# Last batch of an attention kernel: where the output projections of the batch ahead run, and when the last context is read out

## What is computed

```python
xn  = layernorm(x)                       # x: 8 batches x 512 tokens x 512
q, k, v = split(xn @ Wqkv.T + b_qkv)     # 16 heads of 32
p   = softmax(q @ k.T / sqrt(32) + alibi, causal)
s   = (p @ v) @ Wout.T + b_out           # the output projection, per batch
e   = argmax(xn @ w_router.T)            # one of two experts per token
h   = xn @ w_fc[e].T
a   = square(where(h >= 0, h, 0.5 * h))  # hidden 2048
g   = silu(probability * (a @ w_proj[e].T))
out = x + s * g
```

## Time and profile before

| | |
|---|---|
| three runs | 1479.03, 1481.97, 1482.86 us; median 1481.97 |
| profiled execution | 1481.51 us; its span 1479.7 us |
| TensorE busy | 1384.0 us (94%), mean granted clock 0.987 |
| VectorE, ScalarE, GpSimd busy | 923.9 (62%), 770.7 (52%), 682.5 us (46%) |
| attention | to 755.4 us of the span |
| last batch, steps 4 to 15 | 683.9 to 733.2 us |
| last context to first expert product | 733.2 to 755.4 us |
| expert part | 755.4 us to the end |

### The profile page before, as it was taken

One profiled execution on the slowest core, in us unless ns is written; L12 is line 12 of the kernel. 1 busy time (PEld: TensorE's weight loads), 2 busy tenths in 40 slices (PEclk: granted clock), 3 DMA queues, 4 the chain that ended last, 5 costly groups with the idle time before them and its releaser, 6 DMA issues.

```text
span 1479.7 us, 30039 instructions
## 1 busy us (share of the span) xinstructions
PE 1384.0 (94%) x9863; PEld 880.8 (60%) x9863; DVE 923.9 (62%) x2441; ACT 770.7 (52%) x1824; POOL 682.5 (46%) x896
## 2 busy tenths in 40 slices
PE   2889999999999999999689999999999999999995
PEld 1455555655555565555456666666666666666663
DVE  7577777777777777777759745555444555544444
ACT  3478778787777878787736422222222222222221
POOL 0356667465666746566523433333333333323332
PEclk9989999999999999999999999999999999999998
DMA  4425334343534434245346311110011111010100
GB/s 161 144 86 148 125 115 125 110 139 100 171 101 130 128 106 138 89 141 140 107 164 207 115 44 44 44 43 25 23 41 42 39 44 44 30 29 30 36 30 30
DMA packets 84897, 133.45 MB, mean 90 GB/s; under 512 B 14095, under 2 KB 63247, under 8 KB 82576
## 3 DMA queue, kind: packets, MB, share of 16 engines
q1 hardware_dynamic: 75808, 105.70, 23.0%
q0 software_dynamic: 8944, 25.83, 5.6%
HBM read 97.81 MB, written 33.95 MB: 89 GB/s over the span
## 4 chain that ended last, share of the span: by engine, by line
PE 75%; DVE 10%; POOL 6%; ACT 3%; issue 3%; DMA 1%; DVEq 1%; SPq 0%; ACTq 0%; POOLq 0%
PE psY L1126 19%; PE psF L1106 19%; PE psA L352 19%; PE psT L446 7%; PE psA L461 5%; POOL pr L941 4%; PE psS L425 3%; DVE sg L1303 2%; PE psX L1080 1%; POOL route L969 1%; PE psA L409 1%; DVE stat L749 1%; DVE am L636 1%; ACT stage L519 1%; DVE wf L1225 1%
## 5 line engine op out<-in xcount | busy, mean ns | idle before, releaser
L1106 PE MATMUL psF<-xT,wf 128*128 128x256 f16 (+1 forms) x3264 | 368.0, 269 | 0.0
L1126 PE MATMUL psY<-wf,aT 128*128 x1584 | 363.9, 379 | 0.3 <-DVE aT L1270 0.3
L1106 PEld LDWEIGHTS psF<-xT,wf 128*128 x3264 | 312.0, 98 | 63.5
L1344 POOL TENSOR_TENSOR a<-a 128x512 f32<-128x512 f32 (+1 forms) x136 | 153.1, 1126 | 392.1 <-DVE a L1261 390.5
L941 POOL TENSOR_SCALAR pr<-pr,rden 128x128 f32<-128x128 f32 (+3 forms) x512 | 268.4, 542 | 141.9 <-DVE rden L868 140.3
L579 ACT ACTIVATE pr<-pr,mn 128x128 f32<-128x128 f32 (+3 forms) x512 | 281.9, 553 | 0.0
L857 DVE CUSTOM_DVE_ANT_0 pr<-psS,base,nsl 128x128 f32<-128x128 f32 (+3 forms) x512 | 249.6, 543 | 4.2 <-PE psS L425 4.2
L1126 PEld LDWEIGHTS psY<-wf,aT 128*128 128x128 f16 x1584 | 154.5, 98 | 158.5 <-issue 1.0
L446 PE MATMUL psT<-conf,pr 128*128 128x128 f32 x1280 | 205.7, 279 | 18.1 <-POOL pr L941 16.5
L1183 ACT ACTIVATE rl<-psF 128x512 f32<-128x512 f32 (+1 forms) x136 | 79.3, 583 | 263.2 <-PE psF L1106 263.0
L446 PEld LDWEIGHTS psT<-conf,pr 128*128 128x128 f32 x1280 | 157.3, 143 | 81.3 <-POOL pr L941 27.3
(11 more groups left out here) (155 smaller groups left out, 1371.0 us busy)
## 6 DMA issues: line engine op xcount, KB each, us to landing
qk_parts<-pre SPq DMA_DIRECT2D x64, 256.0 KB, 2.8
qs<-qk_parts SPq DMA_DIRECT2D x128, 128.0 KB, 2.7
ks<-qk_parts SPq DMA_DIRECT2D x128, 128.0 KB, 2.7
wst<-in_wf SPq DMA_DIRECT2D x16, 1024.0 KB
wstage<-in_wf SPq DMA_DIRECT2D x32, 512.0 KB, 4.6
xin<-in_x SPq DMA_DIRECT2D x32, 256.0 KB, 4.4
attn_out<-so SPq DMA_DIRECT2D x32, 256.0 KB, 2.0
pt<-in_wqkv SPq DMA_DIRECT2D x4, 768.0 KB, 10.1
```

The costliest lines, as they stand in the source:

```text
L1106: last = nc.tensor.matmul(psF[c % 2][:, k * TT:k * TT + tn], w(e, 2 * hc, hl, kc * 512 + col, P), xT[:, r % 2, x, kc, 0:tn], start=(m == 0 ...
L1126: last = nc.tensor.matmul(psY[r % 2][h][:], aT[:, c % 4, x, k, h * P:(h + 1) * P], w(e, 2 * hc + 1, hl, q * 512, 512), start=(c == 0 and k ...
L1344: nc.gpsimd.tensor_tensor(at, at, at, ALU.mult).then_inc(s["a_ready"], 1)
```

## The change

In the last batch the four projections of the batch ahead run in steps 5, 7, 9 and 11, where they ran in steps 4 to 7. The last batch's context goes to the half of `v` that the batch before it has left (`cx_last`), so its high half no longer waits for those projections. A projection takes high x low before low x high, and waits for the low halves only between its first and last six matmuls. In the iteration behind the last batch ScalarE reads the last context out before the pieces 1 to 5, VectorE writes its high half a step earlier and its low half too (GpSimd did), both ahead of the pieces 1 to 5. The matmul that spreads the weight maxima moves from step 13 to 14, the second transposition of expert tokens from the last step to behind the last context, and the weight scales from the end of step 14 to the start of step 15 (not shown below). The loops over `STEP[step]` on all engines go over `jobs_at(b, step)` instead.

```diff
+LAST_STEP = [(0, 1), (2,), (3,), (4,), (7,), (5,), (), (8,), (15,), (11,), (), (12,), (21,), (), (), ()]
+LAST_ORDER = [p for step in LAST_STEP for p in step]
+def jobs_at(b, step):
+    return LAST_STEP[step] if b == B - 1 else STEP[step]
...
+    cx_last = v[:, B % 2, :, :].rearrange("p q d -> p (q d)").bitcast(F16).rearrange(
+        "p (g x n) -> p g x n", g=NG, x=2)
+    def context(batch):
+        return cx_last if batch == B - 1 else cx
...
         def bank(b, p):
             bb, q = b, p - ABANKS
+            if b == B - 1 and p >= 5:
+                at = LAST_ORDER.index(p)
+                q = [n for n in LAST_ORDER[:at] if n % ABANKS == p % ABANKS][-1]
...
                 if i == 0:
                     wait(pe, s["ctx_hi"], (batch + 1) * NG)
-                    wait(pe, s["ctx_lo"], (batch + 1) * NG)
-                products(ps[:], [(cx[:, g, x, i * P:(i + 1) * P], wout[:, g, a, :])
-                                 for x, a in PARTS for g in range(NG)], mid, s["O_done"])
+                def between():
+                    mid()
+                    if i == 0:
+                        wait(pe, s["ctx_lo"], (batch + 1) * NG)
+                products(ps[:], [(context(batch)[:, g, x, i * P:(i + 1) * P], wout[:, g, a, :])
+                                 for x, a in ((0, 0), (0, 1), (1, 0)) for g in range(NG)], between, s["O_done"])
...
-                if b == B - 1 and step == 13:
+                if b == B - 1 and step == 14:
                     pe.wait_ge(s["fam_row"], 1)
                     nc.tensor.matmul(psA[0][:, 0:2], ones2[:], famd[:], start=True, stop=True
                                      ).then_inc(s["fam_spread"], 1)
-                if b == B - 1 and step >= 14:
-                    ffn["xtrans"](pe, 0, step - 14)
+                if (b, step) in ((B - 1, 14), (B, 0)):
+                    ffn["xtrans"](pe, 0, int(b == B))
...
-                if (b, step) in ((B - 1, 15), (B, 0)):
-                    ffn["split_hi"](act, range(2 * (step == 0), 2 * (step == 0) + 2))
-                if b == B and step in (0, 2):
-                    ffn["turn_hi"](act, 0, step // 2, 0)
-                    ffn["split_hi"](act, range(4 + step // 2, 5 + step // 2))
+                if (b, step) == (B - 1, 15):
+                    ffn["split_hi"](act, range(0, 1))
+                    ffn["turn_hi"](act, 0, 0, 0)
+                if (b, step) == (B, 1):
+                    ffn["turn_hi"](act, 0, 1, 0)
+                    ffn["split_hi"](act, range(1, 6))
...
-                if j == (3 if g else 2):
+                if j == (3 if g else 2 if b < B else 1):
                     if within(pb, 0, B):
                         wait(dve, s["ctx_staged"], pb * NG + pg + 1)
-                        wait(dve, s["O_done"], pb * QB + 1)
-                        nc.vector.tensor_copy(cx[:, pg, 0, :], cf[:]).then_inc(s["ctx_hi"], 1)
+                        if pb < B - 1:
+                            wait(dve, s["O_done"], pb * QB + 1)
+                        nc.vector.tensor_copy(context(pb)[:, pg, 0, :], cf[:]).then_inc(s["ctx_hi"], 1)
+                    if b == B:
+                        dve.wait_ge(s["ctx_hi"], NU)
+                        nc.vector.tensor_tensor(context(pb)[:, pg, 1, :], cf[:], context(pb)[:, pg, 0, :],
+                                                ALU.subtract).then_inc(s["ctx_lo"], 1)
...
                 if b == B - 1 and step == 15:
                     ffn["norm"](dve, 0, 1, 0)
-                    ffn["split_lo"](dve, range(0, 2))
-                if b == B and step == 0:
-                    ffn["split_lo"](dve, range(2, 4))
-                if b == B and step in (1, 3):
-                    ffn["turn_lo"](dve, 0, step // 2, 0)
-                    ffn["split_lo"](dve, range(4 + step // 2, 5 + step // 2))
+                    ffn["split_lo"](dve, range(0, 1))
+                    ffn["turn_lo"](dve, 0, 0, 0)
+                if b == B and step == 1:
+                    ffn["turn_lo"](dve, 0, 1, 0)
+                    ffn["split_lo"](dve, range(1, 6))
...
-                if j == (3 if g else 2) and within(pb, 0, B):
+                if j == (3 if g else 2) and within(pb, 0, B) and b < B:
```

More of the change, by code:

```diff
@@ L248, in jobs @@
     def jobs(b, odd, step, kinds=("q", "k", "v", "x", "o", "logits", "rank")):
-        for p in STEP[step]:
+        for p in jobs_at(b, step):
             kind, db, i = JOBS[p]
@@ L469, in iteration @@
                 ptrans(b, g, j, 0)
-                todo = [p for p in STEP[step] if job_exists(b, p) and JOBS[p][0] != "ctx"]
+                todo = [p for p in jobs_at(b, step) if job_exists(b, p) and JOBS[p][0] != "ctx"]
                 def between():
@@ L860, in masked @@
                         op0=ALU.add, op1=ALU.min, accum_out=mn[:, c:c + 1]).then_inc(s["ttr_done"], 1)
+                if (b, step) == (B - 1, 15):
+                    weight_scales()
                 rb, rh = head_at(b, step + N_LEAD)
@@ L908, in iteration @@
                     ffn["norm"](dve, 0, 0, 0)
-                if b == B - 1 and step == 14:
-                    weight_scales()
                 if b == B - 1 and step == 15:
                     ffn["norm"](dve, 0, 1, 0)
-                    ffn["split_lo"](dve, range(0, 2))
-                if b == B and step == 0:
-                    ffn["split_lo"](dve, range(2, 4))
-                if b == B and step in (1, 3):
-                    ffn["turn_lo"](dve, 0, step // 2, 0)
-                    ffn["split_lo"](dve, range(4 + step // 2, 5 + step // 2))
+                    ffn["split_lo"](dve, range(0, 1))
[3 more added lines that the diff above has]
+                    ffn["split_lo"](dve, range(1, 6))
             assert not more or k[0] == LINKS, k[0]
@@ L958, in iteration @@
                 pb, pg = (b, g - 1) if g else (b - 1, NG - 1)
-                if j == (3 if g else 2) and within(pb, 0, B):
+                if j == (3 if g else 2) and within(pb, 0, B) and b < B:
                     wait(pool, s["ctx_hi"], pb * NG + pg + 1, s["apart_pool"])
-                    nc.gpsimd.tensor_tensor(cx[:, pg, 1, :], cf[:], cx[:, pg, 0, :], ALU.subtract
+                    nc.gpsimd.tensor_tensor(context(pb)[:, pg, 1, :], cf[:], context(pb)[:, pg, 0, :], ALU.subtract
                                             ).then_inc(s["ctx_lo"], 1)
```

## The result

The changed kernel takes 1485.87 us (median of 13 runs, 1483.35 to 1492.04) against 1481.52 for the kernel before, measured beside it: ratio 1.0029, 95% interval 1.0018 to 1.0041, 4.3 us slower. Forecast were 1481.7 in 1477.2 to 1485.2. The profiled execution (1488.1 us, span 1486.3) is one of the slower ones: its first expert product comes at 762.09, 6.7 us behind the 755.36 of the earlier trace rows, and from there to the end both take 724.2 to 724.3 us. So the loss lies wholly ahead of that product, as forecast; its size is what was missed.

A forecast was written before the change was run, and what follows sets the result against it. TensorE-led chain bounds the kernel, via the first expert product's start: last batch +2.2, first projection 5.3 earlier, its clock 2.0 more, bank wait 5.4 back, clock 2.0 back: 755.36 to 755.6, so 1481.51 + 0.2 = 1481.7 us; range 1477.2 to 1485.2.

The forecast's parts named there:

- step 11: Last batch: the projection's read-out holds VectorE 1.2 us more; reciprocals for step 13 at 722.5 instead of 720.27, 2.2 late.
- the clock behind the gap: Last two of the four projections: clock falls after TensorE's wait, costing 2.0 us; bounds nothing to 5.2.
- the gap itself: Before the third projection: TensorE waits 5.4 us for VectorE's read-out, which stands behind the splits of pieces 1 to 5.
- The lead of step 4 and its loss in step 9: Last batch: second context 1.9 us ahead, at 704.7; after step 9's read-out, step 10's reciprocals at 713.6, 0.5 lost.
- the 2.2 of the standing: Last batch: VectorE standing behind read-outs in steps 9 and 11 makes step 13's reciprocals 2.2 us late.
- SyncE is moved past too: Piece loads issued after batch 6's last projection store, not before 720.5 instead of 706.0; cover 3.5 us, so no cost.
- Part 2: Last head to first projection: last context ends at 736.4, first projection starts at 737.75, 5.3 us ahead of 743.01.
- the last batch's 2.2: Term of the sum: the last batch's chain, up to the last transposes, moves 2.2 us later.
- Part 3: Third projection: starts at 748.4 after a 5.4 us wait; lead of 7.2 shrinks to 1.8, clock behind costs 2.0.
- The rivals: Four other outcomes: 1479.5 (chance 0.22), 1474.3 (0.11), 1489.9 (0.05), and 1484 if the change fails to act (0.02).
- the slower one: Steps 5, 7, 9, 11: read-outs hold VectorE a full 2.6 us each, 10.4 late, 1489.9 us; chance 0.05.
- point of decision: Slower rival decides against the change once the batch ends over 2.4 us late; beyond 0.3% from 6.8 on.

The follow-up runs named there:

- loads first: Changed kernel with SyncE issuing the loads of weight pieces 0 to 3 ahead of the stores of the batch ahead: 1480.98 us, ratio 1.0005 to before.
- steps back: Changed kernel with the projections of the batch ahead back in steps 4 to 7, handover still changed: 1477.43 us, ratio 0.9990 to before.
- Reductions apart: Changed kernel, piece 0-3 loads before stores, VectorE's piece 3-5 splits behind projection read-outs, last two weight reductions in steps 8 and 10: 1472.82 us, ratio 0.9940.
- both losses undone: Changed kernel with projections back in steps 4 to 7 and VectorE's splits of pieces 3 to 5 behind its read-outs: 1472.09 us, ratio 0.9953.
- the idle matmuls: Changed kernel with six overwritten matmuls behind each of steps 12 to 14 of the last batch: 1484.61 us, ratio 1.0024 to before.
- loads first and splits behind: Changed kernel with piece 0 to 3 loads ahead of the stores and VectorE's piece 3 to 5 splits behind its read-outs: 1476.80 us, ratio 0.9978.

## Why the prediction was wrong

The mechanism was right nearly step by step; the sum was 6.5 us short in the profiled execution (first expert product forecast at 755.6, seen at 762.1): 1.5 from step 11, 2.4 from the gather, 2.8 from the clock at the last transposes and the context, 0.9 from the clock behind the gap, 1.4 less from the gap itself; 0.3 are small shifts. In the medians it was 4.2 short (1481.7 forecast, 1485.87 measured). One row of the kernel before bears on the clock's part, the transposes of step 14 (the other rows of ten take 1.25 to 1.31):

```profile
726.97 2.40 PE L446 MATMUL psT<-conf,pr 128*128 128x128 f32 x10 [0.27 <-POOL pr L941]
```

- **The lead of step 4 and its loss in step 9**: forecast 704.7 and 713.6, seen 704.52 and 713.46. Right.
- **Step 11**: forecast 2.2 us late at the reciprocals for step 13, seen 3.7. Missing were 0.8 of half clock in the first six products, and some 0.5 of it in the transposes and scores around them. With the clock full there, as in loads first, step 13 is some 2.6 us late, so the 2.2 of the standing were nearly right. I looked for the clock's fall only behind the last context, though the trace of the kernel before shows one in the last batch too, in the transposes of step 14 (2.40 us, the row above). Why it falls in step 11 in one trace and not in another stays open: TensorE's wait in step 10 was 1.42 us before and 1.85 after, but it was 1.86 in loads first too, where the clock stayed at 1.00, and 1.42 in steps back, where it fell to 0.50. Reductions apart shows that the standing hung on the reductions behind the read-outs; their 1.4 us I had counted, but as fixed.
- **"SyncE is moved past too"**: this is the step that failed. I asked whether the loads come in time for their own splits, and they do. I did not ask what they run beside: the gather was to land as soon after its issue as before, and the move of SyncE stood in the sum at nothing. Held back to 724.29, they share the DMA engines with the gather of 727.53, which lands 5.8 instead of 3.4 us after its issue: 2.4 us on the chain to the last transposes. Loads first removes it and wins 0.24%; its ratio, 1.0005, is near the forecast's 1481.7 to 1481.51, though some of that nearness is luck, as the gap was shorter than forecast and the clock fell elsewhere. The Trainium skill ("DMA: Bandwidth & Descriptors", "Issuing engines are not separate DMA queues") says that a DMA from GpSimd's queue and one from SyncE's run on the same DMA engines; the traces agree: 5.8 us beside loads that keep them 0.95 busy, at most 3.8 without them.
- **Part 2**: "731.85 + 2.2 = 734.05, end 736.4". With the chain 4.0 later and the clock at half in the last transposes (1.1 more) and the context (1.7 more), the first projection starts at 744.75, 7.0 behind the forecast. The parts that the change itself made (context ahead of the tokens, read-out ahead of the splits) came as worked out: with both losses undone the first projection is 6.7 us earlier than before, where 7.5 is my sum without the last batch's 2.2.
- **Part 3**: the gap was 4.0, not 5.4 us (the load of piece 5 landed sooner, 3.62 us behind its issue); the clock behind it cost 2.9, not 2.0. That the clock falls there isn't certain in each execution: behind the same gap of 4.0 us two projections took 8.14 us here, 6.93 in steps back, 6.76 in loads first and 5.36 with the idle matmuls. The Trainium skill ("TensorE: Matmul & The Clock Gate", "Why this matters for your kernels") has the clock back at half in such a gap; here it was so in three executions of four, and in the fourth it stayed at 1.00.
- **The rivals**: the slower one named the right place (read-outs that hold VectorE) and put its point of decision at 2.4 us late (by the prediction's own sum it is 2.0, since at 2.2 the change is 0.2 slower already, and 6.4 rather than 6.8 for 0.3%); seen were 3.7 at step 13 and 6.2 at step 15. It got a chance of 0.05 because I priced it only by what VectorE stands, not by what else sits behind those read-outs: stores, loads, the gather, the clock.

The median loss, 4.3 us, is less than the 6.7 of the profiled execution; runs reach from 1483.35 to 1492.04, and the clock's different falls can make 2.8 us of such a spread behind the gap alone (8.14 against 5.36 in two traces with the same gap). Which falls the other runs had isn't known.

## What to carry to other kernels

When a job moves to a later step, list what stands behind its read-out on that engine and behind its store on the DMA queue, and then what these meet when they come late: here a store held four loads back until they ran beside a gather on the critical path. A long instruction of little urgency (here a 1.4 us reduction) does not belong right behind a wait for another engine; two of them moved by one step were worth 0.38% (0.9978 to 0.9940), a part of it through the clock. And a read-out that frees a bank belongs ahead of background work that waits for its own loads.

## What the hardware showed unexpectedly

TensorE's granted clock fell to 0.50 in the last batch where it was busy, if thinly: the changed kernel had it at half in step 11 and for 13 us from step 14 on, behind waits of 1.91 and 1.98 us with 1.3 us of transposes between them; in the kernel before it fell there too (0.65 over 726 to 728, 0.50 over 728 to 730), but was back at 1.00 from 730 on. It isn't the same from trace to trace: after the same wait of 1.86 us in step 10 it stayed at 1.00 in loads first and fell to about 0.57 (mean of 2 us) in loads first and splits behind. Six idle matmuls in each of steps 12 to 14 kept it up through step 14 only. A gather of 256 KB that takes 3.4 us alone took 5.8 us beside 2 MB of loads.
